# One normalisation in place of two chained ones, a residual formed from scales, and a result stored in eight pieces

## The reference, cut to what matters

```
h = h + L1_ffn(layernorm(h))              # layernorm: (h - m) / sqrt(v + 1e-5)

L1_ffn(x):                                 # x is already normalised
    mu, var = mean(x), mean((x - mu)^2)    # and is normalised again
    n = (x - mu) * rsqrt(var + 1e-5) * ln_g + ln_b
    gates = softmax(top 2 of (n @ w_r + b_r))       # 8 experts
    mixed = sum over the 2 picked experts of gate * (gelu(n @ W1 + b1) @ W2 + b2)
    return x + mixed
```

## Time and profile before

| | us |
|---|---|
| median of 3 runs | 1608.4 |
| lowest and highest run | 1603.88, 1612.2 |
| the profiled execution, its own time | 1606.17 |
| its span, first to last instruction | 1604.5 |
| from the first norm's first statistics to the router's first instruction | 381.08 to 401.27 |
| first to last instruction of the last block (the store) | 1598.96 to 1604.5 |

### The profile page before, as it was taken

How to read it: one execution, slowest core, us unless ns; L and a number is a source line. 1 busy time by engine, 2 the same in 40 slices (tenths; PEclk the granted TensorE clock), 3 DMA queues, 4 the chain that set the end, 5 groups by cost and what they waited for, 6 DMA issues and landing times. The chain is left out here.

```text
span 1604.5 us, 29750 instructions
## 1 busy us (share of the span) xinstructions
PE 1141.8 (71%) x10322; PEld 781.8 (49%) x10330; DVE 1158.3 (72%) x2211; ACT 729.9 (45%) x1093; POOL 727.9 (45%) x626
## 2 busy tenths in 40 slices
PE   5857999984489445968777777777777785646770
PEld 3725565663389425744444444444444444435550
DVE  5666556455435447348999999999999995658983
ACT  4233443431045221025777777777767763011540
POOL 2213333231386657123555565555556553215655
PEclk9889999997589777769999999999999986858995
DMA  4052000001168300000000000000000000013772
GB/s 125 1 163 85 2 2 2 2 3 53 40 193 227 98 4 0 0 1 1 1 1 0 0 0 0 0 0 0 0 0 0 0 0 1 2 28 89 211 211 71
DMA packets 83243, 64.92 MB, mean 40 GB/s; under 512 B 13931, under 2 KB 73606, under 8 KB 82886
## 3 DMA queue, kind: packets, MB, share of 16 engines
q1 hardware_dynamic: 62726, 46.80, 10.5%
q0 software_dynamic: 4096, 8.40, 1.8%
q10 hardware_dynamic: 16320, 8.40, 1.8%
HBM read 43.64 MB, written 22.28 MB: 41 GB/s over the span
## 5 line engine op out<-in xcount | busy, mean ns | idle before, releaser
L2118 POOL TENSOR_TENSOR ta_ex<-ta_ex,ta_left 128x1024 f32<-128x1024 f32 x128 | 302.0, 2359 | 279.5 <-ACT ta_left L2061 279.5
L1962 PE MATMUL ta_ps_s<-ta_kT,ta_qz 128*128 (+1 forms) x512 | 258.6, 629 | 36.7 <-ACT ta_ex L2045 35.6
L1993 PE MATMUL ta_ps_t<-consts,ta_ex 128*128 128x128 f32 x1024 | 142.3, 283 | 111.7 <-POOL ta_ex L2118 53.0
L1993 PEld LDWEIGHTS ta_ps_t<-consts,ta_ex 128*128 128x128 f32 x1024 | 113.5, 144 | 176.0 <-POOL ta_ex L2118 137.6
L2149 DVE MAX8 ta_top<-ta_ps_s 128x8 f32<-128x1024 f32 x128 | 156.3, 1221 | 34.3 <-PE ta_ps_s L1962 33.7
L2045 ACT ACTIVATE ta_ex<-ta_ps_s,ta_ntop 128x1024 f32<-128x1024 f32 x128 | 142.7, 1115 | 49.1 <-DVE ta_left L2155 36.7
L2155 DVE MATCH_REPLACE8 ta_left<-ta_top,ta_ps_s 128x1024 f32<-128x1024 f32 x128 | 155.3, 1213 | 0.0
L2160 DVE MAX8 ta_top<-ta_left 128x8 f32<-128x1024 f32 x128 | 154.6, 1208 | 0.0
L2165 DVE MATCH_REPLACE8 ta_left<-ta_top,ta_left 128x1024 f32<-128x1024 f32 x128 | 154.6, 1208 | 0.0
L1962 PEld LDWEIGHTS ta_ps_s<-ta_kT,ta_qz 128*128 128x128 f32 x512 | 89.5, 195 | 119.1 <-issue 104.8
L2061 ACT ACTIVATE ta_left<-ta_left,ta_ntop 128x1024 f32<-128x1024 f32 x128 | 146.3, 1143 | 0.8
(11 more groups left out here) (623 smaller groups left out, 2532.4 us busy)
## 6 DMA issues: line engine op xcount, KB each, us to landing
l1e_w<-in_L_ffn_W_dram SPq DMA_DIRECT2D x46, 256.0 KB
l3e_packed<-l3f_packed SPq DMA_DIRECT2D x64, 160.0 KB, 2.9
l3f_rows<-l1f_zero SPq DMA_DIRECT2D x2, 2048.0 KB, 13.0
l3e_x<-l3f_rows SPq DMA_DIRECT2D x32, 128.0 KB, 2.9
l3e_outs<-l3e_y ACTq DMA_DIRECT2D x32, 128.0 KB, 2.7
l1f_rows<-l1f_zero SPq DMA_DIRECT2D x2, 1472.0 KB, 9.4
l1e_x<-l1f_rows SPq DMA_DIRECT2D x46, 64.0 KB
l1e_outs<-l1e_y ACTq DMA_DIRECT2D x46, 64.0 KB
```

Of the source, the lines that this page charges most:

```text
L1962: ins = pe.matmul(ps_s[:, i % 2, half * BANK:(half + 1) * BANK], qz[:, odd, h, :], kT[:, grp, bass.ds(at.key0[i // PAIR] + half * BANK, BA ...
L1993: ins = pe.transpose(ps_t[:, j * P:(j + 1) * P], ex[:, i % 4, j * P:(j + 1) * P], m.ident)
L2118: pool.tensor_tensor(ex[:, i % 4, :], ex[:, i % 4, :], left[:, i % 4, :], ALU.subtract).then_inc(kept, 1)
```

## The change

- The two norms `ln_l1f` and `ln_l1g` become one block, `l1_norm`. It uses the identity that a row with variance v, once normalised, has mean 0 and variance v/(v+eps), so that the twice-normalised row is (h - m) * ((1+eps)*v + eps^2)^(-1/2). POOL raises two numbers for each row to the power -1/2: that one, and v+eps, the scale of the first norm, in one instruction of 128x16 for each half. Two small DVE operations for each half prepare them.
- The once-normalised rows `xn` aren't formed any more in this part. What the residual needs of them is kept as two numbers for each row in `r.lift`: 1 + rate and mean * rate. At the start of `l1_experts` DVE makes `h * lift0 - lift1` in 16 instructions, one for each tile, in place of one addition of 128x2048.
- The last block with its one store is gone. SP, in `l3_experts`, after its last load, waits for the additions of each pair of tiles (`h_step` of 4, 8, ... 32) and stores the pair, 128 KB, in 8 transfers; it then waits for all eight before the block ends.

```diff
@@ l1_experts, DVE
-            dve.tensor_tensor(m.h[:, :, :], m.h[:, :, :], m.xn[:, :, :], ALU.add).then_inc(xn_added, 1)
+            for t in range(TILES):
+                ins = dve.tensor_scalar(m.h[:, t, :], m.h[:, t, :], r.lift[:, 0, t:t + 1], r.lift[:, 1, t:t + 1], ALU.mult, ALU.subtract)
+            ins.then_inc(xn_added, 1)
@@ stage_l1_ffn
-        layernorm(nc, m, "ln_l1f", m.h, m.xn, None, fetch=fetch)
-        layernorm(nc, m, "ln_l1g", m.xn, r.hn, r.hT, gain=r.ln_g[:, 0:1], shift=r.ln_b[:, 0:1], loaded=(r.s_router, r.n_router))
+        r.W2_dram = w["L1_ffn_W2"]
+        r.lift = sb("lift", [P, 2, TILES])
+        l1_norm(nc, m, r)
@@ l3_experts, SP, after the last load
+            to = m.out.rearrange("b (t p) d -> p (b t) d", p=P)
+            for g in range(TILES // 2):
+                sp.wait_ge(h_step, 4 * g + 4)
+                sp.dma_start(to[:, 2 * g:2 * g + 2, :], m.h[:, 2 * g:2 * g + 2, :]).then_inc(stored, 16)
+            sp.wait_ge(stored, 16 * (TILES // 2))
@@ l1_norm (new), DVE
+            for k, of in enumerate(halves):
+                for t in range(k * CH, (k + 1) * CH):
+                    ins = dve.bn_stats(stats[:, t, :], m.h[:, t, :])
...
+                dve.tensor_tensor(var[:, of], sumsq[:, of], diff[:, of], ALU.add).then_inc(chain, 1)
+                dve.wait_ge(chain, 4 * k + 4)
+                dve.tensor_scalar(wide[:, k, 0, :], var[:, of], 1.0 + EPS, EPS * EPS, ALU.mult, ALU.add)
+                dve.tensor_scalar(wide[:, k, 1, :], var[:, of], EPS, None, ALU.add).then_inc(var_ready, 1)
+            for t in range(TILES):
+                if t % CH == 0:
+                    dve.wait_ge(rate_ready, t // CH + 1)
+                dve.tensor_scalar(r.hn[:, t, :], m.h[:, t, :], mean[:, t:t + 1], rates[:, t // CH, 0, t % CH:t % CH + 1],
+                                  ALU.subtract, ALU.mult).then_inc(normed, 1)
+            for k, of in enumerate(halves):
+                dve.tensor_tensor(r.lift[:, 1, of], mean[:, of], rates[:, k, 1, :], ALU.mult)
+                dve.tensor_scalar(r.lift[:, 0, of], rates[:, k, 1, :], 1.0, None, ALU.add)
@@ l1_norm (new), POOL
+                pool.wait_ge(var_ready, k + 1)
+                pool.tensor_tensor(rates[:, k, :, :], wide[:, k, :, :], half_power, ALU.pow).then_inc(rate_ready, 1)
@@ tower, after the last stage
-        with nc.semaphore("stored") as stored, nc.Block() as block:
-            @block.sync
-            def _(sp):
-                sp.dma_start(out.rearrange("b (t p) d -> p (b t) d", p=P), m.h[:, :, :]).then_inc(stored, 16)
-                sp.wait_ge(stored, 16)
```

More of the change, by code:

```diff
@@ L1553, in stage_l1_ffn @@
         r.w2_in = signals(nc, m, "l1f_")("w2_in")
-        def fetch(sp):
-            sp.dma_start(r.w2_all[:, :, :].rearrange("p e (c d) -> p e c d", c=4),
-                         w["L1_ffn_W2"].rearrange("e (c p) d -> p e c d", p=P)).then_inc(r.w2_in, 16)
-        layernorm(nc, m, "ln_l1f", m.h, m.xn, None, fetch=fetch)
-        layernorm(nc, m, "ln_l1g", m.xn, r.hn, r.hT, gain=r.ln_g[:, 0:1], shift=r.ln_b[:, 0:1], loaded=(r.s_router, r.n_router))
+        r.W2_dram = w["L1_ffn_W2"]
+        r.lift = sb("lift", [P, 2, TILES])
+        l1_norm(nc, m, r)
         router(nc, m, r, "l1r", 8, m.wrT[:, :], 0)
@@ L2413, in l3_experts @@
                              "y_ready"))
+        stored = sem("stored")
         gates_turned, gates_in, bias_ready, bias_added, h_step = (
@@ L2817, in l3_early, with l1_norm, _ @@
     return issue
+def l1_norm(nc, m, r):
+    with ExitStack() as ctx:
+        stats = ctx.enter_context(nc.sbuf_tensor("ln_l1f_stats", [P, TILES, 6], F32))
+        small = ctx.enter_context(nc.sbuf_tensor("ln_l1f_small", [P, 4, TILES], F32))
+        wide = ctx.enter_context(nc.sbuf_tensor("ln_l1f_wide", [P, 2, 2, CH], F32))
+        rates = ctx.enter_context(nc.sbuf_tensor("ln_l1f_rates", [P, 2, 2, CH], F32))
+        ps = ctx.enter_context(nc.psum_tensor("ln_l1f_ps", [P, 4, BANK], F32))
+        sem = signals(nc, m, "ln_l1f_")
+        chain, var_ready, rate_ready, normed, turned, scaled = (
+            sem(x) for x in ("chain", "var_ready", "rate_ready", "normed", "turned", "scaled"))
+        mean, diff, sumsq, var = (small[:, i, :] for i in range(4))
+        halves = [slice(k * CH, (k + 1) * CH) for k in range(2)]
+        block = ctx.enter_context(nc.Block())
+        @block.vector
+        def _(dve):
+            for k, of in enumerate(halves):
+                for t in range(k * CH, (k + 1) * CH):
+                    ins = dve.bn_stats(stats[:, t, :], m.h[:, t, :])
+                ins.then_inc(chain, 1)
+                dve.wait_ge(chain, 4 * k + 1)
+                dve.tensor_tensor(diff[:, of], stats[:, of, 1], stats[:, of, 4], ALU.subtract)
+                dve.tensor_tensor(sumsq[:, of], stats[:, of, 2], stats[:, of, 5], ALU.add)
+                dve.tensor_tensor(mean[:, of], stats[:, of, 1], stats[:, of, 4], ALU.add).then_inc(chain, 1)
+                dve.wait_ge(chain, 4 * k + 2)
+                dve.tensor_scalar(mean[:, of], mean[:, of], 0.5, None, ALU.mult)
+                dve.tensor_scalar(sumsq[:, of], sumsq[:, of], 1.0 / D, None, ALU.mult)
+                dve.scalar_tensor_tensor(diff[:, of], diff[:, of], 0.25, diff[:, of], ALU.mult, ALU.mult).then_inc(chain, 1)
+                dve.wait_ge(chain, 4 * k + 3)
+                dve.tensor_tensor(var[:, of], sumsq[:, of], diff[:, of], ALU.add).then_inc(chain, 1)
[10 more added lines that the diff above has]
+                dve.tensor_scalar(r.lift[:, 0, of], rates[:, k, 1, :], 1.0, None, ALU.add)
+        @block.gpsimd
+        def _(pool):
+            half_power = m.neghalf[:, :].rearrange("p (a t) -> p a t", a=2)
+            for k in range(2):
+                pool.wait_ge(var_ready, k + 1)
+                pool.tensor_tensor(rates[:, k, :, :], wide[:, k, :, :], half_power, ALU.pow).then_inc(rate_ready, 1)
+        @block.sync
+        def _(sp):
+            sp.dma_start(r.w2_all[:, :, :].rearrange("p e (c d) -> p e c d", c=4), r.W2_dram.rearrange("e (c p) d -> p e c d", p=P))\
+              .then_inc(r.w2_in, 16)
+        @block.tensor
+        def _(pe):
+            for t in range(TILES):
+                pe.wait_ge(normed, t + 1)
+                ins = pe.transpose(ps[:, t // 4, (t % 4) * P:(t % 4 + 1) * P], r.hn[:, t, :], m.ident)
+                if t % 4 == 3:
+                    ins.then_inc(turned, 1)
+        @block.scalar
+        def _(act):
+            act.wait_ge(r.s_router, r.n_router)
+            for g in range(TILES // 4):
+                act.wait_ge(turned, g + 1)
+                act.activation(r.hT[:, g * BANK:(g + 1) * BANK], ps[:, g, :], ACT.Identity, bias=r.ln_b[:, 0:1], scale=r.ln_g[:, 0:1])
@@ L2880, in tower @@
         m = Core()
-        m.signals, m.held = [], []
+        m.signals, m.held, m.out = [], [], out
         tower_memory(nc, m, ctx)
```

## The result

| | changed kernel, us | kernel before, us |
|---|---|---|
| first comparison, median | 1591.06 (1589.19 to 1592.23, 4 runs) | 1610.3 (1603.88 to 1613.17, 4 runs) |
| ratio, 95% interval | 0.9872 (0.9827 to 0.9917) | |
| the profiled execution, its own time and its span | 1592.23, 1590.4 | 1606.17, 1604.5 |
| all runs whose granted clock is listed, on several chips: mean | 1601.7 (17 runs) | 1608.8 (56 runs) |
| of these, the runs on the one chip that has both: mean | 1605.0 (13 runs) | 1609.4 (22 runs) |

In the first comparison the changed kernel is 1.3% faster, and its time lies in the forecast range (1593.5; 1586 to 1602). The last two rows came out of the experiments, and they are less: 7.1 us, and 4.4 us where the chip is the same, both under the 8 us of the prediction's bound. Three steps did what the prediction worked out, 14.6 us together.

What follows compares the result with a forecast made beforehand. The bound was taken to change by stage: DVE at the norms, POOL at the experts' start, last gather to store at the end. 7.6 + 1.5 + 5.2 - 0.2 = 14.1 us, from mean 1607.7 to 1593.6; named 1593.5, range 1586 to 1602.

Steps and rivals of the forecast that it cites:

- 8 us of the prediction's bound: Whole kernel: a difference under 0.5%, 8 us, can't be told from none.
- Norms, 7.6: Two norms before the router: one DVE pass in place of two gains 7.6 us, between 6.8 and 8.7.
- First scatter, 1.5: Start of the experts: POOL's first scatter takes 1.1 us in place of 2.68, gaining 1.5 us.
- rival of a first use: First scatter: a program's first indirect transfer may itself cost 1.7 us, so no gain there; scatter rival's chance 0.20.
- short ones let POOL in: Start of the experts: short DVE instructions don't hold POOL up, so the first scatter takes 1.1 us.
- End, 5.2: End of the kernel: eight stores in the expert block in place of one in its own block gain 5.2 us.
- rival that pays it behind the store: End: the block end's 2.4 us comes behind the last store, so the end gains 3.2 us; chance 0.10.
- First stores, -0.2: Last expert block: the first store may meet the last expert outputs; 0.2 us charged, between 0 and 0.8.
- All later stages wait only for what comes before them.: Stages after the changed places: the gain of 14.1 us is expected to be carried to the end.
- clock rival: Expert stream: PE's clock stays lower in 12 or more further blocks, some 2.0 us each; 1615 and more, chance 0.05.

Runs made afterwards that it cites:

- e6: The changed kernel with POOL's powers cut to 128x8, those for the twice-normalised rows of both halves first; one run, 1617.9 us.
- e4: The kernel before with the one addition of xn to h cut into sixteen of 128x128; one run, 1616.52 us.
- e5: The kernel before with the addition of xn to h replaced by four scalings of the whole h, so another result; one run, 1608.63 us.
- e8: The changed kernel without the store of the last two tiles; one run, 1588.79 us.
- e9: The changed kernel, nothing edited, run for a third time; seven runs from 1583.2 to 1620.36 us, median of all seven 1611.56 us.
- e3: The changed kernel, nothing edited, in the same rounds as its two halves; 1609.74 us, ratio 0.9988 to the kernel before.
- g1: The changed kernel with one unused PE product of 256 columns added in most steps of the third layer's feed-forward stage; 1599.66 us, ratio 0.9965 to the kernel before.
- e1: The changed kernel with the last block and its one store as before; 1605.04 us, ratio 0.9985 to the kernel before.

## Why the prediction was right, and where it was short

- **Norms, 7.6.** Measured 7.70. The power of 128x16 took 2.89, estimated at 2.87; DVE's gap 0.73, foretold as 0.8. (From 389.89 and 2.09 us for eight tiles the sum would end at 391.98, not 392.05, and the gain be 7.7.) That POOL is what became late is shown by e6.
- **First scatter, 1.5.** Measured 1.43 on the scatter and 1.34 at the row load. The rival of a first use is refuted by e4. The reason I gave, short ones let POOL in, is true of scalings (0.39 us of delay for e5's 2.19); for additions it is true in small part (1.23 for 1.73), so the number came out right in part because the change also put scalings in an addition's place.
- **End, 5.2.** Measured 5.52. The sum had 0.1 + 2.2 + 0.44 for store and block end in a row. In fact the block's end, 5.5 us behind POOL's last gather, runs beside the store and is last: without the last store (e8) it comes as late. The prediction named this, but left its sum with the store, and that the two sums are nearly the same (2.7 and 2.4 us) is luck. The rival that pays it behind the store (3.2) is refuted.
- **First stores, -0.2.** POOL's wait for the last outputs was 3.85 us for 3.63, 3.65 in e9: 0.2 or nothing.
- **"All later stages wait only for what comes before them."** This is the step that fell short. It is true of the order, but in the third layer's feed-forward stage the time also depends on PE's clock, and the mean clock of the run came out lower (0.854 to 0.868) in 9 of 17 runs of the changed kernel. Two of the nine were profiled (e3, e9), and both have the stage 19 to 22 us longer than in the first profile after. The clock rival had the mechanism, in the wrong place: in the expert stream, whose clock is unchanged. At one clock the gain is 11.9 to 13.4; over all runs it is 7.1, and 4.4 on the one chip that has both. So the four runs of the first comparison, all in the lower group, flatter the change: its 19.2 us of medians are more than the three steps can give, and that the time fell so near 1593.5 is in part their luck.

**Open.** Why runs with the new norm have the falls more often wasn't found. The norms move that stage 7 to 9 us earlier, which wasn't tried by itself. The 15 of 25 against 2 of 22 rest on one chip; the four runs of the first comparison had none. The slope is a relation between time and clock over whole runs, not a measured cost, and what makes the last expert layer vary (201.9 to 211.2 us, with either norm) wasn't taken apart. A version that is surely faster than both wasn't found: g1 is steadier (1596 to 1606, mean 1600.2), but it ran on another chip than the changed kernel did, whose mean is 1601.7, and the two means hardly differ.

## What to carry to other kernels

Read what a step is worth from the one instruction that lets the next stage begin: three such readings, with 0.2 charged for the first stores, gave 14.1, and 14.6 was measured. Then look for a stage in which the granted clock falls for short times and the bounding engine waits for PE at each; two kernels are compared there at the same clock, over many runs on one chip, or the change's own few microseconds drown in it. When the clock of two kernels is compared over a stretch, shift its limits by what the change has moved. Before a transfer at the end is cut up, see what else the end of the block waits for.

## What the hardware did that I had not expected

- Short falls of the granted clock in a stage where PE is busy 76% to 79% (468 to 487 of 613 us): about 1 us each, up to 31 us in a run, and with them two groups of times for one and the same program, their means 18 (e1) to 29 us (e9) apart.
- One added product of 256 columns in most steps held the clock at 1.00, and cost the kernel before about 6 us (ratio 1.0031 and medians 1611.52 to 1605.07).
- A block end 5.5 us behind the last indirect gather in the kernel before, the changed one and e8, with or without a store.
- Long scalings on 128x2048 (1.25 us each) held two scatters up by about a microsecond each; sixteen on 128x128 held three up by 0.4 in all.
